# Self-attention of a decoder layer, regrouped: token quarters outside, head groups inside, output projection over all groups at once

## The chip, the cores and the metric

One core of a Trainium2 chip runs the whole kernel in one launch. The metric is the device time of an execution in microseconds (us). TensorE is PE in the rows, VectorE DVE, ScalarE ACT, GpSimd POOL, SyncE SP.

## What is computed

A post-norm decoder layer on x of 32 sequences x 64 tokens x 512 features (2048 tokens), in three parts, each followed by a layer norm of the sum with its input: self-attention with 32 heads of width 16, cross-attention (32 query heads, 8 key heads of width 128, rotary positions), and a mixture of 16 experts. The change touches the first and the start of the second.

```
q, k, v = x @ Wq.T + bq, x @ Wk.T + bk, x @ Wv.T + bv        # 32 heads of 16
scores  = q k^T / 4, -inf above the diagonal                  # 64 x 64 for each sequence and head
out     = softmax(scores) @ v                                 # back to (tokens, 512)
x       = layernorm(x + out @ Wo.T + bo)
x       = layernorm(x + cross_attention(x, ctx, mask))
x       = layernorm(x + experts(x))
```

## The kernel before

Every fp32 product is made of three fp16 passes: each operand is split into a high part (ACT rounds it) and a low part (DVE, or POOL, subtracts), and `three_pass` (L288 to L290) does high x high, high x low, low x high into one PSUM bank. The 2048 tokens are cut into 4 quarters of 4 tiles of 128; the 32 heads into 4 groups of 8.

`self_attention` runs 16 steps. The head group i is the outer loop, the quarter q the inner one. A step of TensorE (`step`, L835) does, for its group and quarter: the keys K (12 matmuls of 512 columns into bank 0), transposes of the last step's exponentials (`back_p`, L769), the queries Q (bank 1), two more transposes, half of the values (24 matmuls of 128 columns), the scores of head pairs 0 and 1 (`scores`: 2 mask matmuls L814 and 48 of L823 into banks 2 and 3), then for the step before: probabilities x values (`back_pv`, L300, 96 matmuls), a quarter of the values, the transpose of the attention output (`back_turn`, L793), the last quarter of the values, the scores of pairs 2 and 3 into the same banks 2 and 3, and the output projection of the step before (`back_out`, 12 matmuls of 512 columns: 4 token tiles with the 128 features of this group). So each row tile of `acc` is added to four times, once for each group, by DVE (`back_add`, L646).

DVE takes the maximum of a score bank (`most`, L655), subtracts it (`below_most`, L660), ACT exponentiates (L538). `back_norm` (L630, L633) divides by the row sums and writes `at`, for which `back_turn` waits. ACT and POOL spread the high and low values into block form (L584, L472). All order is by hand: each engine's program is written out in Python and the engines meet through semaphores of `Timeline`, on which a wait names an event of a step.

POOL splits the input quarters (L428, L429), and in the steps after it prepares `bound`, a table of 128 x 2048 numbers that the mask of the cross-attention becomes (L2306 loads it, L2309 and L2310 compute). The layer norm of quarter 0 is started in the last steps (12 small POOL operations, L226, and 2 more, L229 and L231, find its factors); its rows are split by POOL and turned by TensorE at the end. Quarter 1 is normed there and turned in the first cross-attention step, quarters 2 and 3 are done in the cross-attention.

After the 16 steps comes a tail: the last step's transposes, `back_pv`, `back_turn` and `back_out`, with the first keys and values of the cross-attention between them (`next_keys`, `next_values`). Then all engines meet at the end of the block. The cross-attention's first step projects four rotated queries; for each of 5 rotations ACT copies, POOL multiplies and adds (L1048, L1053), ACT and DVE split; TensorE's second score product waits for the fifth. The exponentials are scaled on POOL (L1059), and TensorE transposes them in the next step (L1358).

Of the kernel before, what the change touches and what calls it, by code (L numbers as in the profile page):

```python
# [24 lines left out]
P = 128  # L25
# [83 lines left out]
def build(nc, x, xT, cT, maskf, wqT, wkT, wvT, b3, woT, bo, xwq, xwk, xwv, xwo,  # L109
# [3 lines left out]
    with top:  # L113
# [190 lines left out]
        def self_attention(prefetch_ctx, next_front, next_out, s_next_out, next_keys, next_values, ln):  # L304

            NG, FW = H1 // HG, 3 * P
            VW = HD1 + 1
            with ExitStack() as ctx:
                def b(name, shape, dt=F32):
                    return sb("sa_" + name, shape, dt, ctx)  # L310
                raw_f, wf_h, wf_l = (blocks(z, KD)(FW) for z in (raw_front, front_h, front_l))
                raw_o, wo_h, wo_l = raw_out[:, 0:D], out_h[:, 0:D], out_l[:, 0:D]
                stage = [b(f"stage{n}", [P, KD, QT]) for n in range(2)]
                rawb, bias = b("rawb", [P, 3, NG]), b("bias", [P, 3, NG])
                par, caus = b("par", [P, 2]), b("caus", [P, S])
                maskb, identb = b("maskb", [P, 8, S], BF16), b("identb", [P, 2, S], BF16)
                qh, ql = b("qh", [P, QT], F16), b("ql", [P, QT], F16)
                kk, kx = b("kk", [P, 2, QT], F16), b("kx", [P, 2, 2, QT], F16)
                sc = b("sc", [P, 4, TQ, 2, S])
                mx, rs = b("mx", [P, 4, 8]), b("rs", [P, 2, 16, 1])  # L320
                vh, vl = b("vh", [P, TQ, P], F16), b("vl", [P, TQ, P], F16)
# [5 lines left out]
                oh, ol = b("oh", [P, QT], F16), b("ol", [P, QT], F16)  # L327
                rows_h, rows_l = b("rows_h", [P, TQ, D], F16), b("rows_l", [P, TQ, D], F16)
                lower, upper = slice(0, KD * FW), slice(KD * FW, FRONT)
                s_rf, s_ro, s_cn, s_rb = sem("sa_s_rf"), sem("sa_s_ro"), sem("sa_s_cn"), sem("sa_s_rb")  # L330
                s_q0h, s_q0l, s_xq = (sem("sa_" + n) for n in ("s_q0h", "s_q0l", "s_xq"))
                s_st, s_w0 = [sem(f"sa_first{h}") for h in range(2)], [sem(f"sa_weight{n}") for n in range(3)]
                s_late = sem("sa_late_sums")
# [7 lines left out]
                PE = Timeline(sem("sa_pe"), events(["k", "pt0", "pt1", "q", "pt2", "pt3", "s0", "s1", "pv0", "pv1", "oT", "v",  # L341
                                                    "s2", "s3", "w0", "w1", "w2", "w3"]), NG,
                              ["pt0", "pt1", "pt2", "pt3", "pv0", "pv1", "oT", "w0", "w1", "w2", "w3"])
                AC = Timeline(sem("sa_act"), events(["kh", "pe0", "pe1", "ke", "ko", "qh", "pe2", "pe3", "ex0", "oh", "vh", "ex1",
                                                     "vb", "ex2", "ex3"], [(3, "pe3", ["wfh"]), (3, "vh", ["wvh"]), (0, "ex3", ["woh"])]), NG,
                              ["pe0", "pe1", "pe2", "pe3", "oh"])
                DV = Timeline(sem("sa_dve"), events(["kl", "pl0", "pl1", "ql", "pl2", "pl3", "mx0", "sb0", "mx1", "rc0", "no0", "rc1", "no1",
                                                     "sb1", "ol", "vl", "mx2", "w0", "w1", "sb2", "mx3", "sb3",
                                                     "w2", "w3"], [(3, "sb1", ["wfl"]), (3, "w3", ["wvl"]), (0, "w3", ["wol"])]), NG,
                              ["pl0", "pl1", "pl2", "pl3", "rc0", "no0", "rc1", "no1", "ol", "w0", "w1", "w2", "w3"])  # L350
                PO = Timeline(sem("sa_pool"), events(["vb"]), NG)
                freed = {"k": ("w1", 1), "q": ("w0", 1), "v": ("kl", 0)}
                block = ctx.enter_context(nc.Block())

                def gbank(pe, name, st):

                    event, back = ("vl", 1) if name == "k" and (st.i, st.q) == (0, 1) else freed[name]
                    pe.wait_ge(DV.sem, DV.value(event, st, back))
                    return home[name]
# [6 lines left out]
                def turned_in(st, j):  # L366

                    return SB[j - 2] if st.i is None and j >= 2 else PTB[j % 2]

                def group_bias(n, i):  # L370
                    return bias[:, n, bass.ds(i, 1)]

                def back_group(st, i):

                    return NG - 1 if st.i is None else (i + NG - 1) % NG if st.q == 0 else i

                @block.sync
                def _(sp):
                    def front_weights(g):
                        for n, w in enumerate((wkT, wqT, wvT)):  # L380
                            sp.dma_start(raw_f[:, :, n * P:(n + 1) * P],
                                         w.rearrange("(k p) n -> p k n", p=P)[:, :, bass.ds(g * P, P)]).then_inc(s_rf, 16)
                    for h in range(2):
                        sp.dma_start(stage[0][:, 2 * h:2 * h + 2, :],
                                     xT.rearrange("(k p) t -> p k t", p=P)[:, 2 * h:2 * h + 2, 0:QT]).then_inc(s_st[h], 16)
                    for n, w in enumerate((wkT, wqT, wvT)):
                        sp.dma_start(raw_f[:, :, n * P:(n + 1) * P], w.rearrange("(k p) n -> p k n", p=P)[:, :, 0:P]).then_inc(s_w0[n], 16)
                    sp.sem_inc(s_rf, 48)
                    sp.dma_start(raw_o, woT[0:P, :]).then_inc(s_ro, 16)
                    sp.wait_ge(s_pre_v, 3)  # L390
                    for i in range(NG - 1):
                        front_weights(i + 1)
                        sp.wait_ge(DV.sem, DV.value("wol", Step(i, 0)))
                        met(sp)
                        sp.dma_start(raw_o, woT[bass.ds((i + 1) * P, P), :]).then_inc(s_ro, 16)
                        sp.wait_ge(DV.sem, DV.value("wvl", Step(i, 3)))
                        met(sp)
                    next_front(sp, s_rf)
                    sp.wait_ge(DV.sem, DV.value("wol", Step(NG - 1, 0)))
                    next_out(sp)  # L400
                    sp.wait_ge(s_ro, 16 * NG)

                KQ, V = slice(0, 2 * P), slice(2 * P, 3 * P)

                def split_front_hi(act, c):
                    return act.activation(wf_h[:, :, c], raw_f[:, :, c], ACT.Copy, scale=WS)

                def split_front_lo(dve, c):
                    return dve.scalar_tensor_tensor(wf_l[:, :, c], raw_f[:, :, c], WS, wf_h[:, :, c], ALU.mult, ALU.subtract)

                @block.gpsimd
                def _(pool):
# [28 lines left out]
                    for z in (vbh, vbl):  # L441
                        i_ = pool.memset(z[:], 0.0)
# [1984 lines left out]
```

## Time and profile before

| | |
|---|---|
| runs of the kernel before | 1782.42 us median of 3 (1780.18 to 1782.51) |
| span of the profiled execution | 1784.5 us (its own time isn't given beside the span; the span is 2.1 above the median) |
| TensorE busy | 95% (1702.5 us) |
| VectorE, ScalarE, GpSimd busy | 73%, 51%, 52% |
| self-attention, to the first cross-attention matmul | 325.3 us |

A row of the timeline gives start, duration, engine, line, operation, operands and count, and in brackets how long the engine sat idle before it and what ended that. The duration of a matmul includes its way through the array, so the pace of a run of matmuls is the distance between starts. A row of waits gives the sum, the number of times, and the longest.

### The profile page before, as it was taken

Reading aid. Unit: us, or ns where it says so; the run is one execution under the profiler, and the core shown is the slowest. Engines: PE = TensorE matmul, PEld = TensorE weight load, DVE = VectorE, ACT = ScalarE, POOL = GpSimd, SP = SyncE. Lnnn points to the kernel's source line nnn. Section 1 sums busy time; section 2 is a strip of 40 time slices with the busy share of each in tenths; the row PEclk is TensorE's granted clock in tenths of the full one; section 3 lists DMA queues with packets and bytes.
Section 4 is the critical chain, followed back from the end, with each engine's and each line's share of the span. In section 5 each row is a group of like instructions: output and inputs, shape, how many; then the busy total and the mean of one; then the engine's idle time right before and its main releaser. Section 6 shows DMA issues by size and latency. Waiting matters only on the chain. (4 is left out here: it accounts for less than half of the span.)

```text
span 1784.5 us, 38613 instructions
## 1 busy us (share of the span) xinstructions
PE 1702.5 (95%) x15285; PEld 977.4 (55%) x15285; DVE 1295.5 (73%) x2102; ACT 915.0 (51%) x1525; POOL 923.0 (52%) x745
## 2 busy tenths in 40 slices
PE   6999999899999999999999999999889999899996
PEld 3666666455555555555555555555555555455553
DVE  4787889788888888888888888888786444344445
ACT  4565667665546555555455555555742333233334
POOL 7643125463646464646455546455643555455544
PEclk9999999999999999999999999999999999999999
DMA  8720020221313122314122222121166778787658
GB/s 251 178 47 22 8 63 3 65 85 36 130 37 107 66 83 78 107 42 132 53 93 74 72 72 95 37 95 48 60 213 209 153 155 221 216 205 153 118 95 295
DMA packets 84991, 190.62 MB, mean 107 GB/s; under 512 B 10768, under 2 KB 29584, under 8 KB 82768
## 3 DMA queue, kind: packets, MB, share of 16 engines
q1 hardware_dynamic: 61152, 129.67, 21.6%
q0 software_dynamic: 23088, 58.37, 16.0%
q8 instruction: 126, 2.06, 0.5%
q14 instruction: 49, 0.40, 0.1%
q10 hardware_dynamic: 576, 0.11, 0.0%
HBM read 124.91 MB, written 63.21 MB: 105 GB/s over the span
## 5 line engine op out<-in xcount | busy, mean ns | idle before, releaser
L288 PE MATMUL bank<-xhl,front_h 128*128 128x512 f16 x704 | 268.8, 382 | 12.4 <-DVEq L68 11.8
L289 PE MATMUL bank<-xhl,front_h 128*128 128x512 f16 x704 | 268.7, 382 | 0.0
L290 PE MATMUL bank<-xhl,front_l 128*128 128x512 f16 x704 | 268.5, 381 | 0.0
L1048 POOL TENSOR_TENSOR xa_xs<-xa_xs,sn 128x512 f32<-128x512 f32 x160 | 232.3, 1452 | 45.8 <-ACT xa_xs L1100 45.8
L1059 POOL TENSOR_TENSOR xa_sc<-xa_sc,xa_rs 128x1024 f32<-128x1024 f32 x32 | 60.9, 1902 | 374.6 <-DVE xa_rs L1316 374.6
L1053 POOL TENSOR_TENSOR xa_rr<-xa_x,xa_xs 128x512 f32<-128x512 f32 x160 | 233.3, 1458 | 12.7 <-DVE xa_x L1211 0.2
L288 PE MATMUL bank<-out_h,xa_oh 128*128 128x512 f16 x512 | 194.1, 379 | 10.3 <-DVE xa_ol L1193 6.6
L1967 POOL DMA_INDIRECT scratch_y<-raw_front,moe_to x79 | 125.3, 1585 | 150.4 <-DVE mo_zl L2021 120.0
L290 PE MATMUL bank<-out_h,xa_ol 128*128 128x512 f16 x512 | 194.0, 379 | 0.0
L289 PE MATMUL bank<-out_l,xa_oh 128*128 128x512 f16 x512 | 194.0, 379 | 0.0
L1099 ACT ACTIVATE xa_xs<-bank 64x512 f32<-64x512 f32 x160 | 95.1, 594 | 130.3 <-PE bank L290 126.6
L1211 DVE TENSOR_TENSOR xa_x<-bank,cs 128x512 f32<-128x512 f32 x160 | 109.5, 686 | 65.0 <-ACT xa_xs L1100 60.3
L1216 DVE TENSOR_TENSOR xa_rql<-xa_rr,xa_rqh 128x512 f16<-128x512 f32 x128 | 141.5, 1106 | 12.3 <-ACT xa_rqh L1106 11.7
L1156 ACT ACTIVATE xa_sc<-xa_sc 128x512 f32<-128x512 f32 x64 | 40.2, 629 | 205.8 <-DVE xa_sc L1231 205.8
L2006 DVE SCALAR_TENSOR_TENSOR raw_out<-bank,raw_out 128x256 f32<-128x256 f32 x79 | 33.5, 424 | 152.6 <-ACT raw_out L1982 146.5
L288 PE MATMUL bank<-moe_ring,moe_xth 128*128 x316 | 120.3, 381 | 0.0
L289 PE MATMUL bank<-moe_ring,moe_xth 128*128 x316 | 120.1, 380 | 0.0
L290 PE MATMUL bank<-moe_ring,moe_xtl 128*128 x316 | 120.0, 380 | 0.0
L288 PEld LDWEIGHTS bank<-xhl,front_h 128*128 128x128 f16 x704 | 69.2, 98 | 91.2 <-issue 14.2
L290 PEld LDWEIGHTS bank<-xhl,front_l 128*128 128x128 f16 x704 | 69.3, 98 | 84.3 <-issue 2.2
L1203 DVE SCALAR_TENSOR_TENSOR acc<-bank,acc 128x512 f32<-128x512 f32 x128 | 85.8, 671 | 37.7 <-PE bank L290 37.7
L289 PEld LDWEIGHTS bank<-xhl,front_h 128*128 128x128 f16 x704 | 69.2, 98 | 78.3 <-issue 1.7
(307 smaller groups left out, 4589.0 us busy)
## 6 DMA issues: line engine op xcount, KB each, us to landing
xa_rawc<-in_ew SPq DMA_DIRECT2D x32, 768.0 KB, 5.7
moe_ring<-scratch_w SPq DMA_DIRECT2D x16, 1536.0 KB
scratch_w<-xa_chunk_h SPq DMA_DIRECT2D x32, 384.0 KB, 2.3
scratch_w<-xa_chunk_l SPq DMA_DIRECT2D x32, 384.0 KB, 3.3
raw_front<-in_xwq SPq DMA_DIRECT2D x8, 1024.0 KB, 7.9
raw_out<-in_xwo SPq DMA_DIRECT2D x8, 1024.0 KB, 5.4
scratch_y<-acc SPq DMA_DIRECT2D x6, 1024.0 KB, 8.0
acc<-in_x POOLq DMA_DIRECT2D x4, 1024.0 KB, 10.2
```

Of the source, the lines that this page charges most:

```text
L288: pe.matmul(out_ap, ah, bh, start=start and m == 0, stop=False)
L289: pe.matmul(out_ap, ah, bl, start=False, stop=False)
L290: mm = pe.matmul(out_ap, al, bh, start=False, stop=stop and m == n - 1)
L1048: PO.mark(pool.tensor_tensor(xr, xr, sn[:, :].rearrange("p (a s) -> p a s", a=1) .to_broadcast([P, QT // S, S]), ALU.mult), f"sm{r}", st)
L1053: PO.mark(pool.tensor_tensor(rr[r % 2][:, :], x0[r % 3][:, :], xs[r % 3][:, :], ALU.add), f"ra{r}", st)
L1059: PO.mark(pool.tensor_tensor(s4, s4, rs[:, :, :].rearrange("p h (t a) -> p (h t) a", a=1) .to_broadcast([P, 16, S]), ALU.mult), "nm", st)
L1099: act.activation(xs[r % 3][0:64, :], src[64:128, :], ACT.Copy)
L1156: AC.mark(act.activation(s2, s2, ACT.Exp, scale=float(HD2) ** -0.5), f"ex{h}", st, ("ch",) if (i, q, h) == (NG - 1, NQ - 1, 1) else ())
L1203: DV.mark(dve.scalar_tensor_tensor(row, home[f"w{t}"][:, :], 1 / (WS * OS), row, ALU.mult, ALU.add), f"w{t}", st, also)
L1211: DV.mark(dve.tensor_tensor(xr, home_of(r, st)[:, :].rearrange("p (a s) -> p a s", s=S), cs[:, :].rearrange("p (a s) -> p a s", a=1) .to_b ...
L1216: DV.mark(dve.tensor_tensor(rotated(rkl, rql, r), rr[r % 2][:, :].rearrange("p (a s) -> p a s", s=S), rotated(rkh, rqh, r), ALU.subtract), ...
L1967: pool.indirect_dma_start((ya, yb)[t % 2][:, :], bass.IndirectOffsetOnAxis(m.to[:, t:t + 1], 0), y[:, :], None, compute_op=ALU.add).then_i ...
```

## The change

Quarters are now outside and groups inside: step n is quarter n // 4, group n % 4. All four groups' weights stay in SBUF. The output projection of a token tile waits until its quarter has all four groups (the attention outputs are kept in 7 slots) and is then done in one PSUM bank with 12 matmuls and added once; tile 0 comes in step 5, tile 10 in step 15, tile 11 and tiles 12 to 15 behind the steps. Scores go into banks 0 to 3, all four head pairs in one go, once for each step. K and Q take banks 0 and 1, so they wait for the subtractions of the step before. The values go through a fp32 copy that ACT writes (`v32`), and POOL splits it. Tiles 0 to 7 are normed and turned one at a time in the steps; nothing of the layer norm of quarters 0 and 1 is left for later. `bound` is loaded and computed in the first cross-attention step, after its third rotation. In cross-attention's second step the whole of the output weights is split, not one head of it.

```diff
@@ self_attention
-                SB, PTB, PVB = [bank[2], bank[3]], [bank[4], bank[5]], [bank[6], bank[7]]
-                home = {"k": bank[0], "q": bank[1], "v": bank[0], "oT": bank[1],
-                        "w0": bank[1], "w1": bank[0], "w2": bank[6], "w3": bank[7]}
+                SB, PTB, PVB = bank[0:4], [bank[4], bank[5]], [bank[4], bank[5]]
+                home = {"k": bank[0], "q": bank[1], "v": bank[6], "oT": bank[7], "w": bank[6], "tu": bank[7]}
+                def out_tile(n):
+                    return n - W_LAG if W_LAG <= n < STEPS else None
...
+                    def inverse_root(tile, st):
+                        ...
+                        for _ in range(3):
+                            chain(pool.tensor_tensor(t, y, y, ALU.mult))
+                            chain(pool.tensor_tensor(t, t, v, ALU.mult))
+                            chain(pool.tensor_scalar(t, t, -0.5, 1.5, ALU.mult, ALU.add))
+                            chain(pool.tensor_tensor(y, y, t, ALU.mult))
...
+                    for n in range(STEPS):
+                        if tile is not None:
+                            inverse_root(tile, st)
+                        pool.wait_ge(AC.sem, AC.value("v32", st))
+                        chain(pool.tensor_copy(vh[:, :, :], v32[:, :, :]))
+                        chain(pool.tensor_tensor(vl[:, :, :], v32[:, :, :], vh[:, :, :], ALU.subtract))
...
+                    def output(tile, bank_, name, st):
+                        c, tok = tile // TQ, tokens(tile % TQ)
+                        PE.mark(three_pass(pe, bank_[:, :], [(oh[:, slot(c * NG + g), tok], ol[:, slot(c * NG + g), tok],
+                                                              wo_h[:, g, :], wo_l[:, g, :]) for g in range(NG)]), name, st)
...
+                        for h in range(2):
+                            for b2 in range(2):
+                                for j in J4:
+                                    r, q = slice(32 * j, 32 * j + 32), slice(64 * b2, 64 * b2 + 64)
+                                    pe.matmul(SB[j][q, :].rearrange("p (a c) -> p a c", c=S)[:, :, 32 * h:S], identb[r, h, :],
+                                              maskb[r, h, :, 32 * h:S], start=h == 0, stop=False, skip_group_check=True)
...
+                        values(st)
+                        pe.wait_ge(AC.sem, AC.value("ko", st))
+                        pe.wait_ge(DV.sem, DV.value("ql", st))
+                        if n:
+                            pe.wait_ge(DV.sem, DV.value("sb3", st, 1))
+                        scores(st, () if n else ("pv0", "pv1", "w", "oT"))
+                        if n:
+                            tile = out_tile(n)
+                            back_pv(st, ("w",) if tile is None else ())
+                            if tile is not None:
+                                output(tile, home["w"], "w", st)
+                            back_turn(st)
...
+                    output(STEPS - W_LAG, home["w"], "w", done)
+                    back_pv(done)
+                    next_keys(pe)
+                    back_turn(done)
+                    next_values(pe)
+                    for t in range(TQ):
+                        output(3 * TQ + t, last_home[t], f"w{t}", done)
@@ cross_attention
+                            if first and (q, r) == (0, 2):
+                                mask_bound(pool)
-                            heads_left = slice(0, GQ if i else 1)
-                            AC.mark(act.activation(wo_h[:, heads_left, :], raw_o[:, heads_left, :], ACT.Copy, scale=WS), "woh", st)
+                            AC.mark(act.activation(wo_h[:, :, :], raw_o[:, :, :], ACT.Copy, scale=WS), "woh", st)
```

TensorE, from the end of the values of a step of the self-attention to the work on the step before. Before, the scores come in two parts of 50 matmuls, with `back_pv` behind the first (`sa_maskb` is the causal mask, `sa_kx` and `sa_qh`, `sa_ql` keys and queries, `sa_pth` the transposed exponentials, `sa_vbh` the values in block form):

```order
L814 MATMUL bank<-sa_maskb,sa_identb 128x512 [waits sa_dve,sa_act]
L814 MATMUL bank<-sa_maskb,sa_identb 128x512
L823 MATMUL bank<-sa_kx,sa_qh 64x128 x8
L823 MATMUL bank<-sa_kx,sa_ql 64x128 x4
...
L300 MATMUL bank<-sa_vbh,sa_pth 64x34 [waits sa_dve,sa_pool,sa_act]
...
L793 MATMUL bank<-ident,sa_at 128x128 [waits sa_dve]
L793 MATMUL bank<-ident,sa_at 128x128 x3
```

and in the changed kernel:

```order
L834 MATMUL bank<-sa_maskb,sa_identb 64x512 [waits sa_dve,sa_act]
L834 MATMUL bank<-sa_maskb,sa_identb 64x512 x7
L834 MATMUL bank<-sa_maskb,sa_identb 64x8x32 x8
L843 MATMUL bank<-sa_kx,sa_qh 64x128 x16
L843 MATMUL bank<-sa_kx,sa_ql 64x128 x8
...
L300 MATMUL bank<-sa_vbh,sa_pth 64x34 [waits sa_dve,sa_pool,sa_act]
...
L820 MATMUL bank<-ident,sa_at 128x128 [waits sa_dve]
L820 MATMUL bank<-ident,sa_at 128x128 x3
```

Now 112 matmuls of the scores (16 for the mask, 96 of L843) stand in one piece, directly ahead of the 96 of `back_pv`.

GpSimd, at the start of the cross-attention in the changed kernel (`xa_rr` is a finished rotation, `xa_bound` the table; before, the same ten rotation rows stood without the two of `xa_bound`):

```order
L1066 MEMSET xa_zero 128x512
L1087 TENSOR_TENSOR xa_xs<-xa_xs,sn 128x512 [waits xa_s_cn,xa_act]
L1092 TENSOR_TENSOR xa_rr<-xa_x_0,xa_xs 128x512 [waits xa_dve,xa_pool]
...
L1092 TENSOR_TENSOR xa_rr<-xa_x_2,xa_xs 128x512 [waits xa_dve,xa_pool]
L1074 TENSOR_SCALAR xa_bound<-xa_bound 128x2048 [waits xa_mask_in]
L1076 TENSOR_SCALAR xa_bound<-xa_bound 128x2048 [waits xa_bound]
L1087 TENSOR_TENSOR xa_xs<-xa_xs,sn 128x512 [waits xa_act]
L1092 TENSOR_TENSOR xa_rr<-xa_x_0,xa_xs 128x512 [waits xa_dve,xa_pool]
```

The two operations on the table now stand between the third and the fourth rotation, and the first of them waits for its load, which SP issues as the first of the block.

## Rows read from the trace of the kernel before

**Rows 1.** The page, part 1: busy us, share of the span, instructions of each engine.

```profile
PE 1702.5 (95%) x15285; PEld 977.4 (55%) x15285; DVE 1295.5 (73%) x2102; ACT 915.0 (51%) x1525; POOL 923.0 (52%) x745
```

**Rows 2.** Timeline of TensorE over one whole step of the self-attention.

```profile
199.56 0.38 PE L288 MATMUL bank<-xhl,front_h 128*128 128x512 f16 x1
...
202.15 1.04 PE L769 MATMUL bank<-ident,sa_sc 128*128 128x128 f32 x8
203.02 0.38 PE L288 MATMUL bank<-xhl,front_h 128*128 128x512 f16 x1
...
206.49 0.22 PE L288 MATMUL bank<-front_h,xhl 128*128 128x128 f16 x1
...
207.92 0.39 PE L814 MATMUL bank<-sa_maskb,sa_identb 64*128 64x512 bf16 x2
208.24 0.30 PE L823 MATMUL bank<-sa_kx,sa_qh 32*64 32x128 f16 x8
...
209.03 0.21 PE L300 MATMUL bank<-sa_vbh,sa_pth 128*64 128x34 f16 x2
...
210.66 0.23 PE L288 MATMUL bank<-front_h,xhl 128*128 128x128 f16 x1
...
212.46 0.66 PE L793 MATMUL bank<-ident,sa_at 128*128 128x128 f32 x4 [0.95 <-DVE sa_at L633]
212.95 0.22 PE L288 MATMUL bank<-front_h,xhl 128*128 128x128 f16 x1
...
214.83 0.39 PE L288 MATMUL bank<-out_h,sa_oh 128*128 128x512 f16 x1
...
217.43 0.38 PE L288 MATMUL bank<-xhl,front_h 128*128 128x512 f16 x1
```

**Rows 3.** Timeline of VectorE in that step: the last normalisation ahead of the transpose.

```profile
211.98 0.42 DVE L633 TENSOR_TENSOR sa_at<-bank,sa_rs 128x256 f32<-128x256 f32 x1
```

**Rows 4.** Timeline of TensorE: end of step 0, start of step 1, end of step 15.

```profile
26.04 0.59 PE L814 MATMUL bank<-sa_maskb,sa_identb 64*128 64x512 bf16 x2 [3.00 <-DVE sa_sc L660]
...
27.99 0.61 PE L288 MATMUL bank<-xhl,front_h 128*128 128x512 f16 x1
...
33.01 1.04 PE L769 MATMUL bank<-ident,sa_sc 128*128 128x128 f32 x8
...
307.54 1.04 PE L769 MATMUL bank<-ident,sa_sc 128*128 128x128 f32 x8
```

**Rows 5.** TensorE: waits of 0:360, timeline; page part 3 (queue: packets, MB, share).

```profile
PE bank L300 <- issue: 5.9, 4, 2.8
...
176.47 0.23 PE L289 MATMUL bank<-front_l,xhl 128*128 128x128 f16 x1 [1.02 <-issue]
...
q8 instruction: 126, 2.06, 0.5%
```

**Rows 6.** Timeline of TensorE: first matmul of the cross-attention's block.

```profile
325.33 0.38 PE L288 MATMUL bank<-xhl,front_h 128*128 128x512 f16 x1 [0.48 <-DVEq L68]
```

**Rows 7.** Timeline of GpSimd: first and last of 14 operations that find layer-norm factors.

```profile
288.96 0.20 POOL L226 TENSOR_TENSOR shift<-rstd 128x4 f32<-128x4 f32 x1
...
292.62 0.22 POOL L231 TENSOR_SCALAR shift<-shift 128x4 f32<-128x4 f32 x1
```

**Rows 8.** Timeline of GpSimd: the mask table, and the fourth rotation's start.

```profile
126.32 2.20 POOL L2306 DMA_DIRECT2D bound<-in_maskf  x2 [0.30 <-POOL sa_vbl L472]
...
136.35 7.11 POOL L2309 TENSOR_SCALAR bound<-bound 128x2048 f32<-128x2048 f32 x1 [7.83 <-DMA bound<-in_maskf]
143.54 1.92 POOL L2310 TENSOR_SCALAR bound<-bound 128x2048 f32<-128x2048 f32 x1
...
335.21 1.27 POOL L1048 TENSOR_TENSOR xa_xs<-xa_xs,sn 128x512 f32<-128x512 f32 x1
```

**Rows 9.** Timeline of TensorE: the first exponentials of the cross-attention are transposed.

```profile
352.04 1.09 PE L1358 MATMUL bank<-ident,xa_sc 128*128 128x128 f32 x8 [2.80 <-POOL xa_sc L1059]
```

**Rows 10.** VectorE's split of the output weights: duration min/median/max in ns.

```profile
L1253 DVE SCALAR_TENSOR_TENSOR out_l<-raw_out,out_h x8: 1751/2278/2279, 357.7 to 1201.7; 128x2048 f16<-128x2048 f32 x7, 128x512 f16<-128x512 f32 x1
```

More of the change, by code:

```diff
@@ L326, in self_attention @@
                 at = b("at", [P, TQ, P])
[L327 to L331, printed above, removed]
+                oh, ol = b("oh", [P, SLOTS, QT], F16), b("ol", [P, SLOTS, QT], F16)
@@ L574, in step @@
-                        if q == 3 and not last:
-                            AC.mark(split_front_hi(act, V), "wvh", st)
-                        exponentials(st, (1,))
-                        if last and q == 3:
-                            act.wait_ge(s_rf, 48 * (NG + 1))
-                            ln.AC.mark(act.activation(front_h[:, lower], raw_front[:, lower], ACT.Copy, scale=WS), "lower_h", ln.now)
-                        act.wait_ge(AC.sem, AC.value("vh", st))
+                        AC.mark(act.activation(v32[:, :, :].rearrange("p t n -> p (t n)"), home["v"][:, :], ACT.Copy), "v32", st,
+                                ("nr",) if tile is None else ())
@@ L665, in step @@
-                    def step(i, q, last=False):
-                        st = Step(i, q)
-                        early, alone = last and q >= 2, (i, q) == (0, 0)
+                                                  ALU.subtract), f"sb{j}", st, ("ol",) if j == 2 and (st.i, st.q) == (0, 0) else ())
+                    def step(n):
+                        st = step_of(n)
+                        stats = ("st", "ag", "va", "gu")
+                        added, normed, turned = added_tile(n), normed_tile(n), turned_tile(n)
@@ L688, in step @@
-                        if not alone:
+                        most(st, 1)
+                        if n:
                             back_norm(st, 0)
                             back_norm(st, 1)
-                        below_most(st, 1, ("ol",) if alone else ("wfl",) if last and q == 3 else ())
-                        if early:
-                            ln.statistics(dve, q - 2, (3,))
-                        if q == 3 and not last:
-                            dve.wait_ge(AC.sem, AC.value("wfh", st))
-                            DV.mark(split_front_lo(dve, KQ), "wfl", st)
@@ L734, in _ @@
-                    ln.wait(dve, ln.AC, "lower_h")
-                    ln.DV.mark(dve.scalar_tensor_tensor(front_l[:, lower], raw_front[:, lower], WS, front_h[:, lower], ALU.mult,
-                                                        ALU.subtract), "lower_l", ln.now)
-                    ln.inverse(dve, 1, 1)
+                        below_most(st, 3)
+                    for n in range(STEPS):
+                        step(n)
+                    done = Step(None, 0)
+                    back_lo(done, 0)
@@ L744, in _ @@
+                    back_out_lo(done, STEPS - 1)
+                    dve.wait_ge(DV.sem, DV.value("ad3", done))
+                    ln.statistics(dve, 2, range(TQ))
                     for t in range(TQ):
-                        back_add(done, t)
+                        add(3 * TQ + t, last_home[t], f"w{t}", done, f"w{t}")
                 @block.tensor
@@ L875, in _ @@
+                    for n in range(STEPS):
+                        step(n)
                     done = Step(None, 0)
                     back_p(done, (0, 1))
+                    pe.wait_ge(DV.sem, DV.value("sb3", done, 1))
                     back_p(done, (2, 3))
-                    for t in range(2):
-                        pe.wait_ge(s_late, t + 1)
-                        ln.turn(pe, 0, t, home[f"w{t}"], rows_h, rows_l)
-                    back_pv(done, 0)
-                    back_pv(done, 1)
@@ L1135, in step @@
                                                ACT.Copy, scale=1 / WS), "vh", st)
-                        if alone:
-                            for t in range(TQ):
-                                ln.high(act, 1, t, bank[4 + t])
                         rotated_hi(st, 4)
```

698 lines of the change are left out of this document (334 added, 364 removed).

## The prediction

> **What bounds the kernel now.** I read the page first. TensorE is busy 95% of the span, the next engine, VectorE, 73% [rows 1]. So the question for every edit is whether it takes time off TensorE or puts a wait in front of it. Next I read TensorE's timeline over one undisturbed step [rows 2]. From one K to the next it takes 217.43 - 199.56 = 17.87 us: K 2.59, transposes 0.87, Q 2.59 and transposes 0.87, half the values 1.43, mask 0.32, 48 score matmuls 0.79, `back_pv` 1.63, then from 210.66 to 212.46 a quarter of the values and an idle 0.95, the transpose of the output 0.49, the last values and the second scores until 214.83, the output projection 2.60. The 0.95 is the only idle time: TensorE waits for `at`, which VectorE finishes at 211.98 + 0.42 = 212.40 [rows 3], 3.37 after the scores end at 209.03.
>
> Then I compared 15 such steps with what there is: from 27.99 to 307.54 [rows 4] are 279.55 us, while 15 x 17.87 = 268.1. The other 11.5 have two causes. TensorE stalls without waiting for anything the profile shows, 5.9 us in 4 stalls inside `back_pv` and 1.02 just behind it [rows 5]: 6.9 us, and all five come in or right behind the stretch where matmuls are shortest (50 + 96 in 2.74 us, [rows 2]). And it runs at the lower of its two clock levels (1.2, not 2.4 GHz) after some pauses: after the 3.00 idle at 26.04 the K of step 1 and its surroundings take 33.01 - 27.99 = 5.02 where 2.59 is usual [rows 4], 2.4 us lost. I take the fetch of instructions for the cause of the stalls: the instruction queue moved 126 packets of 2.06 MB together, about 16 KB each [rows 5], for 2 x 15285 matmuls and weight loads [rows 1], so about 243 of them to a packet, and a short matmul uses them up fastest.
>
> **The steps after.** TensorE's matmuls of full width stay the same in number. K and Q are 5.18, transposes 1.74, 48 value matmuls 2 x 1.43 = 2.86, less some for one change of shape: 2.8. `back_pv` 1.63, the turn 0.49.
> The scores are 96 matmuls in one piece, now on four row groups at once, not two. By the score row they take 0.79 / 48 = 16.5 ns each; `back_pv` takes 1.63 / 96 = 17.0 ns each though it streams 34 columns and not 128 [rows 2]. Two shapes so different at one pace say that the rate of instructions sets it, so more tiles at once gain nothing: 1.58. The mask is 16 matmuls on eight small tiles in place of 4; 0.32 (all at once) to 0.64 (as twice the old one), I take 0.4. Scores: 2.0 for 2 x (0.32 + 0.79) = 2.22.
> A step is then 5.18 + 1.74 + 2.8 + 2.0 + 1.63 + 0.49 = 13.8, with an output tile (12 matmuls, 2.60) 16.4, and with four fp32 transposes of a normed tile (half of 0.87) 16.9.
> Steps 1 to 4 have no output tile between `back_pv` and the turn, and the turn waits for `at` again: 3.37 after the scores, of which `back_pv` covers 1.63, so 1.7; VectorE also splits weights in steps 1 to 3, which delays it. I take 2.3 for each: 4 x 16.1 = 64.5. Steps 5 to 15: 11 x 16.4 + 8 x 0.44 = 184.1 (the output tile covers the wait). Together 248.6.
> Do others keep up? VectorE drops three of four additions to `acc` and the low values, and gets one tile's statistics. GpSimd gets the split of the values and, for tiles 0 to 7, 14 small operations: from 288.96 to 292.62 + 0.28 they take 3.9 us [rows 7], the start of which is ready some 7 us into a step, and the result is wanted before the next. All of that fits in 16 us. The cover is thin on ScalarE, which has its last exponential between the last subtraction and the next keys; a miss of 0.5 us a step would be 7.
> Step 0 loses the pause of 3.00, since all four banks are filled at once, but K of step 1 waits for a subtraction, about 1.6; with that and without the slow clock behind it step 1 begins at about 25.0, not 27.99.
> Stalls of fetch: the short matmuls now stand 208 in a row, not 146. A packet is some 122 matmuls with their weight loads, 2.0 us at 16.5 ns. The stall of 1.02 [rows 5] then says that fetching one takes about 3, so a packet that lies wholly in the short stretch costs about 1. A packet's start could fall so in 24 of 122 positions before and can in 86 of 122 now; in the long run 8 or more stalls of about 0.9, I take 7 us (an estimate; as much as now, where two were lengthened by other traffic). For slow clock behind stalls and behind the pauses of steps 1 to 4 I add 4. Bounds: 0 and 0, and one stall of 1.2 in each step with the clock lost behind five.
> The Trainium skill, Runtime: NRT & Kernel Launch, section Instruction fetch mechanics, says that instructions come in blocks of 256 and that crossing a block is mostly hidden; by it both terms would be 0 and the time 11 us lower. This trace agrees with the block (16 KB a packet) and not with the hiding (6.9 us).
> End of step 15: 25.0 + 248.6 + 11 = 284.6, against 307.54: -22.9.
>
> **The tail.** Before, 325.33 - 307.54 = 17.8 [rows 4, 6]. Now: transposes 1.74, with waits of about 2.1 for the last exponential and 2.0 for the addition that frees the bank; tile 11 2.60; `back_pv` 1.63; keys 2.59; turn 0.49; 36 value matmuls 2.1; four tiles of outputs 10.4, of which before only a quarter stood here; last addition 0.7 and the barrier 0.5. That is 26.9: +9.1. So the cross-attention begins at 311.5, 13.8 earlier.
>
> **The start of the cross-attention.** The table is loaded within about 10 us of its first issue (126.32 to 136.35), and the third rotation ends about 335.21, 9.9 after the start: it just fits. Then 7.11 + 1.92 and two hand-overs, 9.2 [rows 8], stand in front of the fourth and fifth rotation. TensorE has only the key product to hide it and already waits 2.80 for the exponentials that come out of this chain [rows 9], so nearly all of it counts. Taken off: the high and low parts of quarter 1 leave ScalarE and VectorE here, about 0.5. Added: the split of all output weights, 2.28 for 1.75 [rows 10], 0.5 in the chain to the next `pv`. ScalarE's longer part lies in its own idle time. Sum +9.2; bounds 0 (hidden) and 13 (load late by 3, slow clock behind a pause of 10). What `bound` cost in the steps before, where GpSimd's values came late, is within the 11.5 above.
> The rest (28 more steps of cross-attention, the experts) is unchanged.
>
> **Sum**: -22.9 + 9.1 + 9.2 = -4.6. Against the profiled span 1784.5 that is 1779.9, which stands 2.1 above the median of the runs; the forecast is 1782.4 - 4.6, **1778 us**.
>
> **Rivals.**
> 1. *Instruction fetch starves the longer stretch.* For it: all five stalls are there, the longest is 2.8, and after a pause the clock falls. Against it: four of five were in a stretch that still let most steps through. 15 stalls of 1.2 are 18, and five slow spells at 2.4 are 12: 30 in place of 11, 1797. It decides the sign from about 16 us of both together.
> 2. *Small tiles run side by side and the scores halve.* For it: before only two row groups worked at once. Against it: the equal pace of the two shapes. It would give 16 x 0.79 = 12.6: 1765. The Trainium skill, TensorEngine Tiling (Array Packing), section Theoretical Speedup, gives up to four times for a dimension of 32 or less, which is this rival.
> 3. *Stalls stay out.* Both terms of 11 vanish: 1767.
> 4. *The table's time is hidden*, because the cross-attention's early waits absorb it: 1769.
> 5. *A new wait in each step*: ScalarE or GpSimd late by 0.3 in 15 steps, or the tail longer: nothing is left, 1782.
>
> **How the numbers follow.** The forecast gets 0.38, rival 1 0.22, rival 2 0.08, rival 3 0.08, rival 4 0.06, rival 5 0.18. About 0.2% (3.6 us) is what a measurement of this kernel can tell from no change. The forecast's own range is 1772 to 1786; I give two thirds of it to faster (0.25), with rivals 2 to 4 (0.22) 0.47; the same gets 0.09 of the forecast and most of rival 5, 0.25; slower gets rival 1 and what is left, 0.28. The range of 1766 to 1795 leaves out the ends of rivals 1 and 2.
>
> **What would show it.** In the changed profile: steps 5 to 15 at 16.4 to 16.9; L843 at 16.5 ns each; the turn idle about 2.3 in steps 1 to 4; the block of the cross-attention starting near 311; the two table operations 7.1 and 1.9 and the first exponentials transposed 36 us after that start, not 27. Wrong if `issue` stalls exceed 12 us, if a step runs over 17.5 without one, or if L843 takes under 12 ns.

## The result, and the profile after

| kernel | median of its runs | lowest to highest |
|---|---|---|
| before | 1781.98 us | 1780.18 to 1782.51 |
| changed | 1802.07 us | 1800.23 to 1803.45 |

The ratio is 1.0114 (95% interval 1.01 to 1.0129): the change makes the kernel slower by some 20 us. The forecast was 1778, faster by 4.6, and the time lies outside the range.

The page of the changed kernel, part 1 (busy us, share of the span, instructions), against [rows 1]:

```profile
span 1799.3 us, 39018 instructions
PE 1702.5 (95%) x15461; PEld 976.4 (54%) x15461; DVE 1268.5 (70%) x2048; ACT 915.8 (51%) x1518; POOL 961.5 (53%) x875
```

TensorE is busy to the tenth as long as before, in a span 14.8 us longer. Since the work got less (the scores, below), that already says two things: it stands still more, and some of its work runs at half the clock. The waits of TensorE in the first 360 us (columns: us in all, times, longest):

```profile
PE bank L300 <- issue: 20.9, 14, 4.1
PE bank L843 <- issue: 6.7, 3, 2.6
PE bank L820 <- DVE sa_at L666: 4.5, 4, 1.8
PE bank L834 <- issue: 0.5, 1, 0.5
```

In place of the 5.9 us in 4 stalls called issue of [rows 5] (6.9 with the one beside them, 7.2 with one of 0.28 ahead of the mask of step 0) there are now 28.1 in 18: one of 0.5 in step 0, seven in steps 1 to 5 (18.3 us) and one in each of steps 6 to 15 (9.4 us). The wait for `at` is there in four steps, as forecast. A step without trouble in its first two thirds, TensorE's timeline from one K to the next (start, us, engine, line, operation, operands, count, idle before):

```profile
197.44 0.38 PE L288 MATMUL bank<-xhl,sa_late_h 128*128 128x512 f16 x1
...
200.91 0.38 PE L288 MATMUL bank<-xhl,sa_late_h 128*128 128x512 f16 x1
...
204.37 0.60 PE L870 MATMUL bank<-ident,acc 128*128 128x128 f32 x4
204.81 0.22 PE L288 MATMUL bank<-sa_late_h,xhl 128*128 128x128 f16 x1
...
207.58 0.53 PE L834 MATMUL bank<-sa_maskb,sa_identb 32*64 32x512 bf16 x16
207.93 0.29 PE L843 MATMUL bank<-sa_kx,sa_qh 32*64 32x128 f16 x16
...
208.87 0.21 PE L300 MATMUL bank<-sa_vbh,sa_pth 128*64 128x34 f16 x2
...
212.00 0.20 PE L300 MATMUL bank<-sa_vbl,sa_pth 128*64 128x34 f16 x1 [1.57 <-issue]
...
212.27 0.39 PE L288 MATMUL bank<-out_h,sa_oh 128*128 128x512 f16 x1
...
212.82 0.63 PE L290 MATMUL bank<-out_h,sa_ol 128*128 128x512 f16 x1
...
216.99 0.38 PE L288 MATMUL bank<-xhl,sa_late_h 128*128 128x512 f16 x1
```

Mask 0.35, 96 score matmuls 208.87 - 207.93 = 0.94 (9.8 ns each, not 16.5 as in [rows 2]). Then, nearly at the end of `back_pv`, TensorE idles 1.57 for nothing that the profile shows, and right behind it the matmuls of the output tile take 0.63 in place of 0.38: the lower clock level. The step lasts 19.55; those beside it without slow clock about 17, with a stall in each.

The marks of the stage: step 1, a slow K in step 2, the end of step 15, the start of the cross-attention and its first transposed exponentials, against [rows 4, 6, 9]:

```profile
23.56 0.39 PE L288 MATMUL bank<-xhl,front_h 128*128 128x512 f16 x1 [1.49 <-DVE sa_sc L701]
...
44.17 0.63 PE L288 MATMUL bank<-xhl,sa_late_h 128*128 128x512 f16 x1
...
302.42 1.04 PE L798 MATMUL bank<-ident,sa_sc 128*128 128x128 f32 x8
305.47 1.32 PE L798 MATMUL bank<-ident,sa_sc 128*128 128x128 f32 x8 [2.02 <-DVE sa_sc L701]
308.63 0.58 PE L288 MATMUL bank<-out_h,sa_oh 128*128 128x512 f16 x1 [1.84 <-DVE acc L678]
...
331.16 0.38 PE L288 MATMUL bank<-xhl,front_h 128*128 128x512 f16 x1 [1.22 <-DVEq L68]
...
366.97 1.09 PE L1390 MATMUL bank<-ident,xa_sc 128*128 128x128 f32 x8 [0.75 <-POOL xa_sc L1100]
```

Step 1 begins 4.4 us earlier than before and step 15 ends only 5.1 earlier; K of steps 1, 2, 3, 4 and 5 begins at 23.56, 44.17, 65.77, 85.50 and 107.16, 20.9 apart where the forecast had 16.1. The tail takes 331.16 - 302.42 = 28.7 (before 17.8), and from the cross-attention's start to the exponentials it is 35.8 (before 26.7). How TensorE's clock stood, from the view by windows (columns: window, length, TensorE busy and its instructions, granted clock, DMA share, GB/s), first of the kernel before, then of the changed one:

```profile
20.00:110.00 90.00, 80.50 (x1338) 0.91 0.65 161
110.00:200.00 90.00, 84.99 (x1496) 0.98 0.13 29
200.00:290.00 90.00, 85.00 (x1501) 1.00 0.11 32
```

```profile
20.00:110.00 90.00, 68.06 (x1323) 0.83 0.57 146
110.00:200.00 90.00, 83.26 (x1578) 0.98 0.17 43
200.00:290.00 90.00, 84.62 (x1593) 0.98 0.08 26
```

0.83 means that a third of those 90 us ran at 1.2 GHz. The loss sits in the first steps: there the changed kernel idles and runs slowly, and there the DMA engines are busy. They were as busy there before the change (0.65), so the traffic alone isn't what is new.

The mask table, timeline of GpSimd, against [rows 8]:

```profile
341.62 7.11 POOL L1074 TENSOR_SCALAR xa_bound<-xa_bound 128x2048 f32<-128x2048 f32 x1 [0.55 <-DMA xa_bound<-in_maskf]
348.81 1.90 POOL L1076 TENSOR_SCALAR xa_bound<-xa_bound 128x2048 f32<-128x2048 f32 x1
```

### The profile page after: what moved, and what is told of

Same layout as the page of the kernel before. It is cut to its first block and busy times, and to the rows that moved or that the text cites. A ratio compares the mean times of both kernels' runs of the same rounds, so it can differ in the third digit from the quotient of the medians.

```text
span 1799.3 us, 39018 instructions
## 1 busy us (share of the span) xinstructions
PE 1702.5 (95%) x15461; PEld 976.4 (54%) x15461; DVE 1268.5 (70%) x2048; ACT 915.8 (51%) x1518; POOL 961.5 (53%) x875
## 5 line engine op out<-in xcount | busy, mean ns | idle before, releaser
L288 PE MATMUL bank<-xhl,front_h 128*128 128x512 f16 x640 | 246.0, 384 | 12.5 <-DVE front_l L643 9.8
L289 PE MATMUL bank<-xhl,front_h 128*128 128x512 f16 x640 | 245.6, 384 | 0.0
L290 PE MATMUL bank<-xhl,front_l 128*128 128x512 f16 x640 | 245.3, 383 | 0.0
L1253 DVE TENSOR_TENSOR xa_rql<-xa_rr,xa_rqh 128x512 f16<-128x512 f32 x128 | 144.7, 1131 | 18.4 <-ACT xa_rqh L1147 17.8
L2009 ACT ACTIVATE raw_out<-bank 128x256 f32<-128x256 f32 x79 | 30.3, 384 | 156.3 <-PE bank L290 156.3
L288 PEld LDWEIGHTS bank<-xhl,front_h 128*128 128x128 f16 x640 | 63.3, 99 | 84.7 <-DVE xhl L636 9.8
L1147 ACT ACTIVATE xa_rqh<-xa_rr 128x512 f16<-128x512 f32 x128 | 80.6, 630 | 52.9 <-POOL xa_rr L1092 52.5
```

The source lines that it names most:

```text
L288: pe.matmul(out_ap, ah, bh, start=start and m == 0, stop=False)
L289: pe.matmul(out_ap, ah, bl, start=False, stop=False)
L290: mm = pe.matmul(out_ap, al, bh, start=False, stop=stop and m == n - 1)
L1147: AC.mark(act.activation(rotated(rkh, rqh, r), rr[r % 2][:, :].rearrange("p (a s) -> p a s", s=S), ACT.Copy), f"h{r}", st, also)
L1253: DV.mark(dve.tensor_tensor(rotated(rkl, rql, r), rr[r % 2][:, :].rearrange("p (a s) -> p a s", s=S), rotated(rkh, rqh, r), ALU.subtract), ...
```

## The experiments

| run | median us | ratio to before, 95% interval |
|---|---|---|
| e1, values between | 1794.73 | 1.0075 (1.0052 to 1.0098) |
| e2, table on VectorE | 1794.66 | 1.0076 (1.0051 to 1.0101) |
| e3, scores in pairs | 1799.97 | 1.0105 (1.0077 to 1.0133) |
| e4, e1 and e2 | 1788.62 | 1.0036 (1.0021 to 1.0051) |
| e5, of the kernel before | 1783.21 | 1.0009 (0.9995 to 1.0023) |
| e6, rows in sixteenths | 1798.15 | 1.0092 (1.0071 to 1.0113) |
| e7, e4 and e6 | 1786.56 | 1.0028 (1.0016 to 1.0041) |
| e8, e7 and a tile between PV halves | 1805.06 | 1.0118 (1.0089 to 1.0147) |
| e9, e6 issued before the split | 1792.66 | 1.0069 (1.0051 to 1.0087) |
| e10, e7 issued before the split | 1776.08 | 0.9971 (0.9961 to 0.9981) |
| e11, e9 and e2 | 1784.21 | 1.0020 (1.0010 to 1.0031) |

The kernel before ran beside them at 1782.48 (e1 to e4), 1782.54 (e5 to e8) and 1781.40 (e9 to e11). The code cuts below show the main lines of each edit; ` ...` stands for lines left out.

### e1: is it the length of the stretch of short matmuls?

Two of the four value tiles go between the scores and `back_pv`.

```diff
-                        values(st)
+                        values(st, range(2))
 ...
-                        scores(st, () if n else ("pv0", "pv1", "w", "oT"))
+                        scores(st)
+                        values(st, range(2, TQ), () if n else ("pv0", "pv1", "w", "oT"))
```

> The changed kernel, with two of the four value tiles of each step (24 matmuls) moved from ahead of the scores to between the scores and back_pv; nothing is added or dropped. Theory F (the instruction supply: 208 short matmuls in a row use up fetched instructions faster than they come): the issue stalls of TensorE in the first 360 us fall from 27.6 us (20.9 at L300, 6.7 at L843) to about 8, most slow-clock stretches of the self-attention go with them, and the time falls from 1802 to 1776 to 1785. Rival W (the new waits of the one-piece scores and of K and Q on the score banks cost the time): the stalls may move but the time stays within 4 us of 1802.

7.3 us under the changed kernel: neither of the two ranges. The waits of TensorE in the first 360 us:

```profile
PE bank L300 <- issue: 14.9, 11, 3.7
PE bank L290 <- issue: 4.8, 1, 4.8
PE bank L844 <- issue: 0.8, 3, 0.4
```

From step 6 on the stalls shrank to 0.2 to 0.8 each (2.9 us in all, from 9.4), but five of 2.9 to 4.8 us stayed, one in each of steps 1 to 5 (17.3, from 18.3). The length of the stretch explains the late stalls; the early ones need something more.

### e2: the mask table

The two operations on `bound` move from GpSimd to VectorE, behind the layer-norm factors in the first cross-attention step.

```diff
-                            if first and (q, r) == (0, 2):
-                                mask_bound(pool)
 ...
                             ln.inverse(dve, 2, 2)
+                            mask_bound(dve)
```

> The changed kernel, with the two operations on the mask table moved from GpSimd (between its third and fourth rotation) to VectorE (behind its fifth cosine product of the first cross-attention step). Theory T (the table sits in the chain of rotations): the first exponentials are transposed about 28 us after the block's start in place of 35.8, and the time falls by 7 to 10 to 1792 to 1795. Rival (that chain is covered by TensorE's other work or by the load of the table): within 2 us of 1802.

7.4 us less, as expected of a chain on the path. VectorE takes 1.22 and 2.17 us for what takes GpSimd 7.11 and 1.90, and the first exponentials are transposed 359.35 - 330.26 = 29.1 us after the start of the block, 6.7 sooner than in the changed kernel:

```profile
343.73 1.22 DVE L1213 TENSOR_SCALAR xa_bound<-xa_bound 128x2048 f32<-128x2048 f32 x1
344.98 2.17 DVE L1215 TENSOR_SCALAR xa_bound<-xa_bound 128x2048 f32<-128x2048 f32 x1
...
359.35 1.09 PE L1389 MATMUL bank<-ident,xa_sc 128*128 128x128 f32 x8 [1.68 <-POOL xa_sc L1090]
```

### e3: are four score banks at once worth anything?

The 96 score matmuls in the order of pairs: banks 0 and 1, then 2 and 3; all else as changed.

```diff
-                        for t in range(TQ):
+                        for js in ((0, 1), (2, 3)):
+                            for t in range(TQ):
 ...
-                                    for j in J4:
+                                        for j in js:
```

> The changed kernel, with the 96 score matmuls of a step issued as head pairs 0 and 1, then 2 and 3 (48 each, two row groups at once) in place of all four at once; the mask matmuls, the banks and all else stay. Both theories: the 96 go from 0.94 us back to about 1.6 us, 10 us more of matmul time over 16 steps. Theory F: the slower pace gives the fetch that time, so the issue stalls fall from 27.6 to about 17 and the time stays at 1799 to 1805. Rival W: the stalls stay and the time rises to about 1812.

The scores of a step took 1.30 in place of 0.94 (13.5 ns each; 1.6 was expected), so four at once are faster, by 0.36 x 15 = 5.4 us in steps 1 to 15. (Before the change the same two row groups took 16.5 ns, in pieces of 48; where those 3 ns went no run separates.) The time didn't get worse (2.1 us less, inside the spread): the stalls went from 28.1 to 23.7. Most of what the faster scores gain, TensorE spends waiting just behind them.

### e4: both at once

> Both edits of the first two runs on the changed kernel: two value tiles between the scores and back_pv, and the table on VectorE. Theories F and T together: 17 to 26 and 7 to 10 us less than 1802, so 1768 to 1778, below the kernel before (1782). Rival W with a hidden table: 1798 to 1802.

1788.62: the two gains add (7.3 + 7.4 = 14.7 by the single runs, 13.5 found). The time is 10.6 above the range of 1768 to 1778, because the early stalls stayed, as in e1.

### e5: the same cut in the kernel before

```diff
                         scores(st, (0, 1))
+                        values((2,))
                         back_pv(st, 0)
                         back_pv(st, 1)
-                        values((2,))
```

> The kernel before, with one edit: in each step the third value tile is computed between the first two score banks and the PV matmuls, so that the run of short matmuls is cut by 0.7 us of longer ones. Fetch theory (TensorE stands still where 256 recorded instructions have gone by faster than their next piece of code arrives): the stalls called issue in the first 360 us, 6.9 us in the kernel before, fall to under 3 us, and the time by 2 to 7 us, to 1775 to 1780. Rival (the cut costs as much as it gives, since PV waits for nothing and the tile was needed where it stood): the time stays within 2 us of 1782.

Nothing gained, and the forecast of stalls under 3 us failed: they went from 6.9 to 5.1, and the wait for `at` rose from 10.2 us in 12 to 14.9 in 16, because the value tile had covered it. In the kernel before, the stretch costs too little for this cut to pay.

### e6: is it the DMA traffic?

Rows and bias come into `acc` one tile per step, 256 KB each, over 16 steps, not 1 MB each in the first five.

```diff
-                        pool.dma_start(acc[:, n * TQ:(n + 1) * TQ, :], rows).then_inc(s_a[n], 16)
+                        pool.dma_start(acc[:, n:n + 1, :], rows).then_inc(s_a[n], 16)
 ...
-                        if n < NQ:
-                            rows_in(n)
-                        if 0 < n <= NQ:
-                            add_bias(n - 1)
+                        rows_in(n)
+                        if n:
+                            add_bias(n - 1)
 ...
```

> The changed kernel, with the input rows and the bias brought into the accumulator one tile per step (256 KB each, over all 16 steps) in place of one quarter per step (1 MB each, in the first 5 steps). Theory Q (the stalls of steps 1 to 5 are the long ones, 2.4 to 4.1 us against 1.4 us later, because the code for TensorE comes through DMA engines that the big transfers keep busy): the five long stalls fall to about 1.5 us each and fewer slow-clock spells follow, 8 to 15 us less in the first 130 us: 1787 to 1794. Rival S (steps 1 to 5 lack the output tile between their short matmuls, and the queues matter little): within 3 us of 1802.

The first steps did as the theory says, the total didn't. K of step 6 began at 111.91 in place of 129.38, 17.5 us earlier, and then three quarters of it were given back: the total fell by 3.9 only, and 1798.15 is in neither range. Here is the view by windows for the 2 us ahead of stalls (the last two columns: share of the DMA engines, GB/s). First the kernel before, ahead of its longest stall of 2.85, then the changed kernel, ahead of stalls of 2.61, 4.07, 2.43, 2.74 and 3.39 us, then of two late ones of 1.20 and 1.57:

```profile
77.30:79.30 2.00, 2.00 (x125) 1.00 1.09 121
```

```profile
33.00:35.20 2.20, 2.19 (x96) 1.00 0.88 318
56.30:58.30 2.00, 1.96 (x153) 1.00 1.11 228
76.50:78.50 2.00, 1.99 (x119) 1.00 1.05 301
99.90:101.90 2.00, 1.91 (x128) 1.00 1.04 191
118.30:120.30 2.00, 1.91 (x139) 1.00 1.10 182
140.10:142.10 2.00, 1.95 (x137) 1.00 0.03 8
208.50:210.50 2.00, 1.94 (x140) 1.00 0.04 8
```

In e6, the same places of steps 2 to 5, ahead of stalls of 1.05, 1.00, 1.17 and 0.85:

```profile
53.60:55.60 2.00, 1.94 (x153) 1.00 0.03 8
69.70:71.70 2.00, 2.00 (x119) 1.00 0.25 46
88.60:90.60 2.00, 1.99 (x159) 1.00 0.03 8
104.80:106.80 2.00, 1.97 (x140) 1.00 0.10 19
```

At the same places of the code a stall behind busy DMA engines is two to four times as long. The pairing isn't perfect: a stall of 1.70 in step 4 of the changed kernel had a share of 1.08 ahead of it, and the second stall of step 1 rose from 1.31 to 1.89 in e6, behind quiet engines. In the steps after, four of ten (6, 8, 10 and 12) got a second stall: 15.4 us in steps 6 to 15, not 9.4. In each of those four the sixteenths landed 0.1 to 1.6 us after the scores had begun.

### e7 and e8: three edits, and one cut more

e7 is e4 and e6 together.

> Three edits of the changed kernel at once: two of the four value tiles between scores and PV, the mask table on VectorE, the rows and bias in sixteenths. If each long stall of steps 1 to 5 hangs on busy queues (theory Q): 1788.6 of the first two edits together, less 8 to 15: 1774 to 1781, at or under the kernel before (1782). If not (rival S): 1786 to 1791.

1786.56, only 2.1 under e4 and in the range of the rival: the traffic, spread over all steps, now meets the short matmuls of the late ones (2.04, 2.87 and 2.42 us of stall in steps 8, 10 and 12, with a DMA share of 0.82, 0.94 and 0.97 ahead). e8 also puts the fourth value tile between the halves of `back_pv`:

```diff
                             PE.mark(mm, f"pv{h}", st, also if h else ())
+                            if h == 0 and between is not None:
+                                between()
 ...
```

> As the run with the three edits, and the fourth value tile stands between the two halves of PV, so that no stretch holds more than 112 short matmuls. By the fetch theory what stalls are left in steps 1 to 15 shrink again: 2 to 6 us less than the run with three edits. By the rival (what is left is the latency of a fetch, which a stretch cut again doesn't hide) within 1.5 us of it.

A plain miss: 18.5 us slower than e7. In e8 stalls of 2.3 to 3.0 us stood inside the scores and `back_pv` of steps 3 to 12, and ahead of four of them the windows show (the fifth row is the one ahead of its last stall):

```profile
67.70:69.70 2.00, 1.92 (x128) 1.00 0.97 264
104.40:106.40 2.00, 1.94 (x107) 1.00 0.91 213
163.60:165.60 2.00, 1.93 (x110) 1.00 0.97 256
203.60:205.60 2.00, 1.96 (x109) 1.00 0.89 216
305.10:307.10 2.00, 2.00 (x140) 1.00 0.03 8
```

The last, with quiet queues, was followed by a stall of only 0.5. The reading: the values end later, GpSimd splits them later and issues its transfers later, so that more of them meets the next step's short matmuls. The traces bear it out. In steps 8, 10 and 12 of e7 the bias of the tile is issued 3.6 to 4.1 us ahead of the scores and lands 1.4 to 2.3 after they begin; in e8 it is issued 2.5 ahead and lands 3.9 to 4.4 after. No run moved the transfers of e8 alone. The stalls went from 18.3 to 25.4, and the granted clock of 110 to 200 and of 200 to 290 from 0.97 and 0.95 to 0.91 and 0.89, which is 0.12 x 90 = 10.8 us more: together at most 17.9 of the 18.5.

### e9, e10, e11: the transfers out of the way

GpSimd issues the sixteenths ahead of its split of the next input half, some 5 us earlier in each step:

```diff
+                        rows_in(n)
+                        if n:
+                            add_bias(n - 1)
 ...
                         if n < len(HALVES):
                             split(n)
-                        rows_in(n)
-                        if n:
-                            add_bias(n - 1)
 ...
```

> The changed kernel with rows and bias in sixteenths, each pair issued by GpSimd ahead of its split of the next half (about 5 us earlier in each step than in the run with sixteenths alone), so that these 0.5 MB have landed before the short matmuls of the step. Theory Q (a transfer under way lengthens a fetch, wherever it comes from): the run with sixteenths had two stalls of 1.1 and 1.8 us in many steps after the fifth, where the changed kernel has 1.4 and 0.6; they come back to those, 6 to 10 us with the slow clock after them: 1788 to 1793. Rival S (the place of the transfers is indifferent, the spells of half clock fall as they fall): within 3 us of the 1798.2 of that run.

> The same issue ahead of the split, with the two edits on values and mask table as well. Theory Q: 4 to 9 us under the 1786.6 of the three edits: 1777.5 to 1782.5, no slower than the kernel before. Rival S: within 2 us of 1786.6.

> As the run just described, without the move of two value tiles. What the move is worth once the transfers are out of the way: by the fetch theory, still 4 to 8 us (two runs of 16 + 96 and 96 short matmuls need less of the fetch than one of 208), so 1783 to 1790 and slower than with it; by the rival (each stretch pays a stall of its own, with the split the total is the same) within 2 us of the run with it.

In e9 and e10 the bias of each tile lands 3.2 to 7.5 us before the scores begin (steps 2 to 14), where e6 had it within 1.6 us of them. e9 is 5.5 under e6, and its stalls sum to 17.8 us, not 22.9. They didn't go back to 1.4 and 0.6 (steps 6, 8 and 10 still have two, of 0.3 to 0.4 and 1.6 to 2.2), so the detail was off. e10 beats every other kernel: 1776.08, 0.9971 of the kernel before, 1.4% under the changed one and a little under its own range. Its stalls sum to 11.9. e11 against it says that the value tiles are worth 8.1 us once the traffic is quiet; e11 against e9, that the table is worth 8.5. e10's waits of TensorE in 0:360, the start of its cross-attention and its first transposed exponentials, and its first window:

```profile
PE bank L300 <- issue: 5.4, 11, 1.8
PE bank L844 <- issue: 5.1, 3, 1.8
```

```profile
309.70 0.38 PE L288 MATMUL bank<-xhl,front_h 128*128 128x512 f16 x1 [1.22 <-DVEq L68]
...
338.21 1.97 PE L1391 MATMUL bank<-ident,xa_sc 128*128 128x128 f32 x8 [2.57 <-POOL xa_sc L1092]
```

```profile
20.00:110.00 90.00, 78.77 (x1655) 0.96 0.34 96
```

The self-attention ends at 309.70, 15.6 us earlier than in the kernel before and 21.5 earlier than in the changed one.

## Why the prediction was wrong

Two of its own signs of being wrong came: stalls called issue over 12 us (28.1), and L843 under 12 ns (9.8).

- **Step 1 at 25.0**: it began at 23.56, with a wait of 1.49 where 1.6 was written. Right, 1.4 early.
- **Steps without trouble**: 16.4, or 16.9 with a normed tile, forecast. When its stall is taken off, 15.9 is left of steps 6 and 15 and 16.3 of most steps between (17.87 before the change). The faster scores should have given 15.7 and 16.2, so the rest was priced 0.1 to 0.2 too low. The wait for `at` came in steps 1 to 4 only, with 4.5 us in all where 4 x 2.3 stood.
- **"More tiles at once gain nothing: 1.58"**: failed. Matmuls of 32 rows and 64 columns of the array went at 9.8 ns with four row groups at work, 13.5 with two (e3). I had taken the equal pace of two shapes for a limit on the issue of instructions; it was none. Rival 2 had the mechanism: from two to four row groups gave 13.5 / 9.8 = 1.4. The Trainium skill, TensorEngine Tiling (Array Packing), section Theoretical Speedup, states it with a factor up to four. It was worth nothing as placed (e3).
- **"I take 7 us" and "I add 4", the term of the fetch stalls and the slow clock**: this is the step that failed. The stalls were 28.1 us, 27.6 of them in steps 1 to 15, not 7. The slow clock: from step 1's start to the end of step 15 the changed kernel took 278.9. Fifteen steps at the pace of an undisturbed one (13.3 for steps 1 to 4, which have no output tile, 15.9 for steps 5, 6 and 15, 16.3 for steps 7 to 14) are 231.3, the waits for data 5.1 and the stalls 27.6; 14.9 are left. The granted clock gives as much at most: 0.17, 0.02 and 0.02 x 90 in the three windows are 18.9, less what fell into idle time. So about 15 us of slow clock (an estimate), not 4: together 43 where 11 stood. The faster scores (15 x 0.7 = 10.5 less than priced) and the shorter waits for `at` (4.7 less) hid 15 of these 32. Two things went into the low price. I let a piece of code cost 1 us when it fell in the short stretch, on the strength of one stall of 1.02, and set aside the long ones as "lengthened by other traffic", without asking whether that traffic was there in the changed kernel as well: it was, 8 MB of rows and bias in the first five steps, and the longer stretch now met it in each of them. And I counted a piece's positions as if they fell at random and got 8 or more stalls; there were 17 in 15 steps. (A piece is 256 recorded instructions, see below, not 243.) Rival 1, with 15 stalls of 1.2 and five slow spells at 2.4 (1797), was the case; there were 18 stalls of 1.56 on average.
- **The tail**: 28.7 for 26.9, with waits of 2.02 and 1.84 where 2.1 and 2.0 stood. Most of the +1.8 is slow clock behind the second wait: the first seven matmuls of tile 11 started 0.42 apart (308.63 to 311.56), not 0.22, which is 1.4 more.
- **The table**: from the block's start to the exponentials 35.8 against 26.7, +9.1 where +9.2 was forecast. The place was right; that the size fits to 0.1 is partly luck. e2, which takes the table out of GpSimd's chain, won 6.7 of the 9.1 there and 7.4 of the time. The rest isn't the table: the granted clock of that stretch was 0.81 (before 1.00, e2 0.94), which the sum had at nothing.
- **The sum**: the stage was to begin its cross-attention at 311.5. It began at 331.16, 19.7 late: stalls and clock, less the faster scores and shorter waits. With the stalls down to 11.9 us it begins at 309.70 (e10). A new wait in each step (rival 5) did not come. The missing 4.6 of the 24 us are no part of the kernel's path: the profiles say +14.8 (1784.5 to 1799.3), the medians +20.1. The span of the changed kernel lies 1.8 under the time of its own run, so the profiled run of the kernel before took about 1786.3 (an estimate), 4 above the median from which the forecast was taken.

The Trainium skill, Runtime: NRT & Kernel Launch, section Instruction fetch mechanics, says that crossing a block of instructions is mostly hidden. The trace disagrees for short matmuls in a long row: here the crossings cost 27.6 us in steps 1 to 15.

## What to carry to other kernels

An engine that issues two instructions each 10 to 20 ns can outrun its own code, and no wait for data names it: look for idle time called issue in the densest stretch, and multiply it before you make that stretch longer. Ask of each big transfer whether it falls ahead of such a stretch; splitting and issuing it earlier, parting the stretch with value tiles, and a table moved off the path turned a loss of 20 us into a gain of 5. A faster operation directly ahead of such a stall gained nothing here (e3).

## What the runs showed of the hardware

- Of the 18 stalls called issue in the changed kernel, 17 (all but one of 0.5 us in step 0), and five of the six of the kernel before, lie 256 recorded TensorE instructions (matmuls and weight loads) apart, or a multiple of it, and each ends 1.2 to 1.6 us after a 16 KB packet of the instruction queue has landed. The packet took 0.9 to 1.6 us. In steps 6 to 15 of the changed kernel, with quiet DMA engines, it began 1.0 to 2.0 us before TensorE stood still; ahead of the five stalls of 2.4 to 4.1 us it began 0.1 to 1.8 us after, and took 0.9 to 1.0. What is late behind traffic is the start of the packet, not its transfer.
- The longest stalls have the highest DMA share in the 2 us ahead of them: with 0.8 to 1.1 they were 1.7 to 4.8 us long (changed kernel, e1, e7, e8), with 0.3 to 0.7 they were 1.0 to 1.8 (e10), with 0.25 and less mostly 0.5 to 1.9. It isn't the only cause: e9 had one of 2.17 with a share of 0.03 ahead of it.
- In steps 1 to 15 of the changed kernel the granted clock fell to 1.2 GHz six times: behind four of the five stalls of 2.4 to 4.1 us, in the course of the fifth (2.74), and behind only one of the ten shorter ones of steps 6 to 15 (1.57). Matmuls then take 0.63 us in place of 0.38; K of step 2 and its transposes took 49.90 - 44.17 = 5.73 where 3.47 is usual. Six such spells cost about 15 us (an estimate, above), 2.5 each.
- One instruction with two comparisons on 128 x 2048 fp32 took GpSimd 7.11 us and one with a multiply and an add 1.90; on VectorE they took 1.22 and 2.17. Which of the two is dear depends on the engine.
